# The first block of the second layer in a two-layer graph kernel: six columns by TensorE ahead of the loop, nineteen by gather, and another order of the vector engine's first steps

## The reference, cut to what matters

```python
# layer 0: an edge network
ew  = (efeat @ W_e + b_e).reshape(E, in_f, out_f)
msg = einsum('ei,eio->eo', feat[src], ew)
neigh = segment_sum(msg, dst) / maximum(cnt, 1) + bias
x = layernorm(x + neigh)
# layer 1: a typed message and a GRU
msg = einsum('emh,eh->em', edge_emb[edge_type].reshape(-1, 16, 16), x[src])
m = segment_sum(msg, dst)
x = layernorm(x + gru(m, x))
```

## Time and profile before

| | |
|---|---|
| median of 3 runs | 4953.85 us (4951.73 to 4953.85) |
| the profiled execution's own time | 4951.33 us |
| its span, first to last instruction | 4949.5 us |
| mean granted TensorE clock | 0.995 |
| busy: PE, VectorE, ScalarE, GpSimd | 4801.9, 4057.1, 4048.1, 3499.9 us |
| layer 0, then the change of layers, then layer 1 | to about 2466, to about 2516, to the end |

### The profile page before, as it was taken

How to read it: one execution, slowest core, us unless ns; L and a number is a source line. 1 busy time by engine, 2 the same in 40 slices (tenths; PEclk the granted TensorE clock), 3 DMA queues, 4 the chain that set the end, 5 groups by cost and what they waited for, 6 DMA issues and landing times.

```text
span 4949.5 us, 133716 instructions
## 1 busy us (share of the span) xinstructions
PE 4801.9 (97%) x40480; PEld 4330.9 (88%) x40481; DVE 4057.1 (82%) x5504; ACT 4048.1 (82%) x5764; POOL 3499.9 (71%) x3682
## 2 busy tenths in 40 slices
PE   6999999999999999999979999999999999999997
PEld 5888888888888888888869999999999999999997
DVE  8888888888888888888867777777777777777776
ACT  7888888888888888888658888888888888888885
POOL 7777777777777777777666767676767676767674
PEclk9999999999999999999989999999999999999999
DMA  3221221221111211112221111111111111111111
GB/s 75 35 37 34 37 35 35 37 34 35 37 34 35 37 34 35 37 34 35 33 34 28 27 28 27 28 27 28 27 28 27 28 27 28 27 28 27 28 27 16
DMA packets 371461, 159.41 MB, mean 32 GB/s; under 512 B 232707, under 2 KB 370531, under 8 KB 371291
## 3 DMA queue, kind: packets, MB, share of 16 engines
q1 hardware_dynamic: 254584, 127.93, 11.4%
q0 software_dynamic: 116672, 30.10, 7.8%
q10 hardware_dynamic: 160, 0.80, 0.1%
HBM read 155.84 MB, written 2.66 MB: 32 GB/s over the span
## 4 chain that ended last, share of the span: by engine, by line
PE 84%; DVE 10%; issue 4%; DVEq 1%; POOL 1%; DMA 0%; ACT 0%; SPq 0%; POOLq 0%; ACTq 0%
PE psN L703 66%; PE psM L733 13%; DVE z L900 4%; DVE cand L871 4%; PE psTR L724 1%; PE psTR L728 1%; PE psTR L725 1%; DVE z L875 1%; PE psTR L713 1%; POOL z L461 1%; DVE grp_hot L862 0%; PE psTR L717 0%; PE psTR L714 0%; DVEq L874 0%; PE psN L816 0%
## 5 line engine op out<-in xcount | busy, mean ns | idle before, releaser
L703 PE MATMUL psN<-table_hi,pick 128*128 128x320 f32 (+1 forms) x13020 | 3879.7, 315 | 45.9 <-DVEq L843 31.2
L703 PE MATMUL psN<-table_lo,pick 128*128 128x320 f32 (+1 forms) x13020 | 3769.9, 305 | 0.0
L703 PEld LDWEIGHTS psN<-table_hi,pick 128*128 128x128 f32 x13020 | 2447.5, 188 | 224.4 <-issue 171.9
L703 PEld LDWEIGHTS psN<-table_lo,pick 128*128 128x128 f32 x13020 | 2450.2, 188 | 0.0
L461 POOL DMA_INDIRECT z<-in_x,idx x1885 | 1798.6, 954 | 658.2 <-issue 471.4
L461 POOL DMA_INDIRECT z<-h_rows,idx x1761 | 1682.9, 956 | 708.5 <-issue 475.9
L520 ACT ACTIVATE dist<-src_mod,neg_node 128x640 bf16<-128x640 uint16 (+1 forms) x2480 | 2000.0, 844 | 64.8 <-ACT pick L528 54.8
L528 ACT ACTIVATE pick<-dist,one 128x640 fp32r<-128x640 bf16 (+1 forms) x2480 | 2003.9, 846 | 23.0 <-PE psN L703 6.8
L900 DVE TENSOR_TENSOR z<-psD,z 128x2048 f32<-128x2048 f32 (+1 forms) x750 | 1367.4, 1823 | 102.2 <-issue 57.9
L871 DVE TENSOR_TENSOR cand<-psN,grp_hot 128x640 f32<-128x640 f32 x1364 | 1075.8, 789 | 434.4 <-PE psN L703 364.8
L875 DVE TENSOR_REDUCE z<-cand 128x32 f32<-128x640 f32 x1364 | 1077.6, 790 | 132.0
(11 more groups left out here) (107 smaller groups left out, 681.4 us busy)
## 6 DMA issues: line engine op xcount, KB each, us to landing
src_mod<-src_mod_rows SPq DMA_DIRECT2D x372, 160.0 KB
z<-in_x,idx POOLq DMA_INDIRECT x1885, 2.3
z<-h_rows,idx POOLq DMA_INDIRECT x1761, 2.3
eab<-in_edge_attr SPq DMA_DIRECT2D x125, 200.0 KB
src_mod<-src_mod_rows SPq DMA_DIRECT2D x124, 192.0 KB
idx<-in_src SPq DMA_DIRECT2D x250, 12.5 KB
dstb<-in_dst SPq DMA_DIRECT2D x250, 14.0 KB
grp<-src_grp SPq DMA_DIRECT2D x248, 5.5 KB, 1.6
```

What stands on the lines that cost most here:

```text
L703: mm = pe.matmul(rows[:, :, 0:cells.shape[2]], pick[j][:, c, at:at + P], cells, start=(i == 0 and part == 0), stop=(i == TC - 1 and part = ...
```

## The change

Layer 1's block 0 no longer gathers all of its columns. The picks of turns 5 to 10 (`PICKED[5:11]`: columns 14, 21, 22, 23, 24 and 20, six of them) are made by TensorE; turns 0 to 4 are still passed over, and their five columns are gathered with the other fourteen: nineteen gathers in place of 25. The diff's `MADE_0` is the number of turns passed over. SyncE loads the source numbers for it (`load_first`) after the last block of layer 0 is picked. ScalarE's `begin()` makes `pick1` of block 0 in place of `pick0` of block 1, which moves to the head of layer 1's `first_body`. TensorE does the six turns of block 0, then eight turns of block 1 (`FIRST_S` goes from 11 to 8), `sum_block(0)`, and three more turns. VectorE does `group_hot` of block 0 and `split_table` ahead of `match_block`, then four selects of block 0, `group_hot` of block 1, and fewer selects of block 1 between the `outer` parts. `H`, `HCUT`, `PAIRS`, `GATHERED` and the `AFTER` tables are now given by buffer as well as by layer, with equal values for both; the counts that the loops wait for are worked out by `ahead`, `picked_of` and `cand_of`. Layer 0 keeps its schedule.

```diff
-H = (10, 11)
+H = ((10, 10), (11, 11))
-FIRST_S = (8, 11)
+FIRST_S = (8, 8)
+HALF_1 = 5
+MADE_0 = (H[0][0], HALF_1)
+FIRST_GATHERED = [[[g for g in range(START[j], START[j + 1]) if g not in PICKED[m:h[0]]] for j in range(NS)] for m, h in zip(MADE_0, H)]
+FIRST_PAIRS = [(5, 6), (6, 8), (8, 10)] + ([(10, 11)] if H[1][0] == 11 else [])
...
+        def ahead(k, buf, r):
+            return sum(H[k]) * r + buf * H[k][0]
+        def picked_of(k, buf, r, n):
+            return ahead(k, buf, r) + H[k][1] + n
+        def cand_of(k, buf, r, n):
+            return ahead(k, buf, r) + RING + n
...
+            def load_first():
+                at = slice(HALF_1 * P, H[1][0] * P)
+                sp.dma_start(src_mod[0][:, at], mod_dram[0:1, at].rearrange("a n -> (a n)").partition_broadcast(P)).then_inc(s_first, 16)
+                sp.dma_start(grp[0][:], grp_dram[0:1, :].rearrange("a (p t) -> (a p) t", p=P)).then_inc(s_first, 16)
...
             load_src(1, 1, 1)
+            sp.wait_ge(L[0]["pick_act"], TC * NH * NB + 1)
+            sp.wait_ge(L[0]["hot_g"], NB)
+            load_first()
             sp.wait_ge(s_agg[0], 1)
...
-                        for g in range(START[j], START[j + 1]) if whole else GATHERED[k][j]:
+                        for g in (FIRST_GATHERED[k] if first else GATHERED[k][buf])[j]:
...
-                                    pool.wait_ge(l["picked"], H[k] * (b + 1) + AFTER_OWN[k][n] + 1)
+                                    pool.wait_ge(l["picked"], picked_of(k, buf, r, AFTER_OWN[k][buf][n] + 1))
...
                 def begin():
                     if k == 0:
                         copy_coef(0, 0, 0)
-                    whole_half(1, 1, 0, 0)
+                        whole_half(1, 1, 0, 0)
+                    else:
+                        whole_half(0, 0, 0, 1)
 
                 def first_body():
+                    if k == 1:
+                        whole_half(1, 1, 0, 0)
                     whole_half(1, 1, 0, 1)
...
                 def first_body():
                     pe.wait_ge(s_split, k + 1)
+                    for t in range(MADE_0[k], H[k][0]):
+                        pick_rows(0, 0, 0, t)
                     for t in range(FIRST_S[k]):
-                        pick_rows(1, 1, t)
+                        pick_rows(1, 1, 0, t)
...
-                    dve.wait_ge(l["picked"], H[k] * (b + 1) + t1)
+                    dve.wait_ge(l["picked"], picked_of(k, buf, r, t1))
...
-                    dve.wait_ge(l["cand"], H[k] * b + t1 + RING)
+                    dve.wait_ge(l["cand"], cand_of(k, buf, r, t1))
...
                     else:
+                        group_hot(0, 0, 0)
+                        split_table(1)
                         match_block(0, 0, 0)
+                        for t0, t1 in FIRST_PAIRS:
+                            select(0, 0, 0, t0, t1)
                         group_hot(1, 1, 0)
-                        split_table(1)
+                        outer(0, 0, 0, 0)
                         selects(0)
-                        outer(0, 0, 0, 0)
-                        selects(1, 2)
                         outer(0, 0, 0, 1)
-                        selects(3, 4)
+                        selects(1)
                     outer(0, 0, 0, 2)
                     dve.sem_inc(l["rel_x"], 1)
                     dve.sem_inc(l["match_x"], 1)
-                    selects(*(range(2, len(PAIRS[k])) if k == 0 else range(5, len(PAIRS[k]))))
+                    selects(*range(2, len(PAIRS[k][1])))
...
-                dve.sem_inc(l["picked"], 2 * H[k])
-                dve.sem_inc(l["pick_act"], TC * NH + 1)
+                halves = NH if k == 0 else 1
+                dve.sem_inc(l["picked"], picked_of(k, 0, 0, MADE_0[k]))
+                dve.sem_inc(l["pick_act"], TC * halves + 1)
```

More of the change, by code:

```diff
@@ L21 @@
 PICKED = [4, 5, 6, 7, 13, 14, 21, 22, 23, 24, 20]
-H = (10, 11)
-HM = max(H)
-SCUT = [[sum(p < START[j] for p in PICKED[:h]) for j in range(NS + 1)] for h in H]
-HCUT = ((0, 5, 10), (0, 5, 11))
+H = ((10, 10), (11, 11))
+HM = max(max(h) for h in H)
+SCUT = [[[sum(p < START[j] for p in PICKED[:h]) for j in range(NS + 1)] for h in hs] for hs in H]
+HCUT = [[(0, 5, h) for h in hs] for hs in H]
 NH = 2
@@ L29 @@
 FILL = 24
-FIRST_S = (8, 11)
+FIRST_S = (8, 8)
 S_AT, T_AT, R_AT = (4, 1), (5, 3), (6, 5)
[L32 to L36, removed]
+GATHERED = [[[[g for g in range(START[j], START[j + 1]) if g not in PICKED[:h]] for j in range(NS)] for h in hs] for hs in H]
+assert all(2 * n % RING == 0 and n >= max(hs) for n, hs in zip(TURN, H))
+HALF_1 = 5
+MADE_0 = (H[0][0], HALF_1)
+FIRST_GATHERED = [[[g for g in range(START[j], START[j + 1]) if g not in PICKED[m:h[0]]] for j in range(NS)] for m, h in zip(MADE_0, H)]
+FIRST_PAIRS = [(5, 6), (6, 8), (8, 10)] + ([(10, 11)] if H[1][0] == 11 else [])
+assert all(c[1] == HALF_1 for c in HCUT[1])
+PAIRS = [[[(t, min(t + 2, h)) for t in range(0, h, 2)] for h in hs] for hs in H]
+AFTER_OWN = ([{3: 0, 5: 1, 6: 2, 7: 3, 8: 4, 12: 5, 13: 6}] * 2, [{5: 0, 6: 1, 9: 2, 10: 3, 11: 4, 12: 5}] * 2)
+AFTER_LAST = ([{1: 8, 2: 9}] * 2, [{1: 7, 2: 8, 3: 9, 4: 10}] * 2)
 SUB = 4
@@ L444, in gathers, with body @@
                 l = L[k]
-                def body(b, buf, r, whole=False):
+                def body(b, buf, r, first=False):
                     pool.wait_ge(l["idx"][buf], 16 * (r + 1))
@@ L464, in body @@
                             ).then_inc(l["got"][buf][j], 16)
-                body(0, 0, 0, whole=True)
+                body(0, 0, 0, first=True)
                 with pool.Fori(0, (NB - 1) // 2) as i:
@@ L684, in bank, with pick_rows @@
                     return (TURN[k] * buf + t) % RING
[L686 removed]
+                def pick_rows(b, buf, r, t):
+                    j = max(j for j in range(NH) if HCUT[k][buf][j] <= t)
+                    at = (t - HCUT[k][buf][j]) * P
                     if t >= RING:
[L689 to L696 removed]
+                        pe.wait_ge(l["cand"], cand_of(k, buf, r, t - RING + 1))
+                    else:
+                        last = max(u for u in range(H[k][1 - buf]) if (u - t - TURN[k]) % RING == 0)
+                        pe.wait_ge(l["cand"], cand_of(k, 1 - buf, r - 1 + buf, last + 1))
                     for i, c in enumerate(CHUNKS):
@@ L760, in first_body @@
                     sum_block(0)
-                    for t in range(FIRST_S[k], H[k]):
-                        pick_rows(1, 1, t)
+                    for t in range(FIRST_S[k], H[k][1]):
+                        pick_rows(1, 1, 0, t)
                     flush_transposes(first)
@@ L987, in body @@
                         outer(*nxt, 1)
-                    selects(*range(3, len(PAIRS[k])))
+                    selects(*range(3, len(PAIRS[k][1 - buf])))
                     if more2:
```

62 lines of the change are left out of this document (31 added, 31 removed).

## The result

The changed kernel takes 4941.0 us (median of 12 runs, 4939.95 to 4942.86); the kernel before, on the same chips, 4953.98 us (median of 12, 4950.91 to 4957.92). The ratio is 0.9974, 95% interval 0.9966 to 0.9983: 13.0 us faster. The forecast was 4949.7 us, the range began at 4945.5, and a gain over 0.2% had 2%. So it was wrong, in size. The profiled executions are 4951.33 and 4942.38 us, spans 4949.5 and 4940.6: 8.95 us apart. The one of before lies 2.65 us under its median, the one of after 1.38 us over its own; together these make the missing 4.0 us. The experiments ran on other chips, in three groups; beside them the kernel before had medians of 4953.65, 4953.88 and 4953.92 us, so the groups can be compared within some 0.3 us.

What follows compares the result with a forecast made beforehand. Gathers bounded layer 1's start up to block 1's sum; afterwards VectorE's closing work would, bringing that sum from 2556.52 to 2552.4. Gain 4.1 us, 4.2 with rounding: 4953.85 - 4.2 gives 4949.7 us, range 4945.5 to 4954.5.

Steps and rivals of the forecast that it cites:

- The head of the stage: VectorE at layer 1's start: split begins 1.27 us earlier, ends at 2514.5; TensorE's first pick at 2514.7.
- The turns: TensorE's fourteen turns before block 0's sum: 4.4 us at half clock, ending 2537.3; register loads add 0.5 us.
- VectorE's tail: VectorE's work after turn 9 of block 1, the new bound: 9.9 us, block 1's sum at 2552.4, 4.1 us earlier.
- Rival (a): Layer 1's start: gathers stay the bound and all 7.5 us arrive, 4946.3 us; chance 14%.
- (b): Layer 1's start: six added turns and selects cost what the gathers gave, 4953.9 up to 4955 us; chance 18%.
- this case: The main forecast for layer 1's start: gain 4.1 to 4.2 us, 4949.7 us, alone 4947.5 to 4951; chance 61%.
- ScalarE: `begin` takes 8.8 us in place of 7.3, covered by 4 us; block 1's `pick1` close, costed at nothing, at most 1 us.
- GpSimd and the split: Gathers beside VectorE's table split: 2.1 us slowdown left in place; by the port rule, nothing to 4.7 us.
- The clock in the gaps: TensorE's wait before block 1's sum: about 3.5 us; if the clock doesn't fall, 1.4 us more saved.
- The step that failed: Layer 1's two-block loop: bounded by TensorE and VectorE, its period and register operations unchanged by the change.
- rival (c): Loop waits for `picked` and `cand` each need one more register operation: 15 us slower, 4964.7 us; chance 4%.
- Rival (d): Layer 1's loop, moved in memory by new code, is fetched again each pass: 30 us slower, 4980 us; chance 1%.

Runs made afterwards that it cites:

- dense table: Window counts copied once into a dense table of 16-bit words and read from there: 5016.57 us on the changed kernel, 5025.75 us on the kernel before.
- one and three signals ahead: Changed kernel with strided 16-bit reads, plus one or three unused VectorE signals before the first block: 5016.92 us and 5024.9 us.
- strided table: Here the kernel before, with strided 16-bit reads and block 0's five surplus part-2 gathers counted on their own semaphore: 5019.79 us.
- The pair with the surplus gathers apart: Kernel before with dense 16-bit table, without and with block 0's five surplus part-2 gathers on their own semaphore: 5025.75 and 5020.97 us.

## Why the prediction was wrong, point by point

**The head of the stage: the order right, the start 1 us late.** The split was to end at 2514.5 and the first pick to start at 2514.7; the pick started at 2515.77. The timeline of VectorE of after has the new order, but 1 us later than I had it:

```profile
2510.47 0.37 DVE L895 TENSOR_TENSOR grp_hot<-col_f,grp 128x220 f32<-128x220 f32 x1
2510.76 1.69 DVE L870 CAST table_hi<-table 128x1280 fp32r<-128x1280 f32 x2
2512.49 3.01 DVE L872 TENSOR_TENSOR table_lo<-table,table_hi 128x1280 fp32r<-128x1280 f32 x2
```

In before `group_hot` started at 2510.72 behind `match_block`; here the copies of the node table that precede it ended 1.0 us later (in this execution TensorE's granted clock was also at half from 2492.5 to 2495.9 us, where before had it full), which ate 1.0 of the 1.27. The profile of before was itself an early one for the gathers: its first gather of layer 1 starts 40.2 us behind the last part-2 multiplication of layer 0, in the other three profiles with the old start 41.2 to 42.7 us. One reading of the earlier trace rows was also too short. The chain of before isn't gathers alone up to the sum of block 1; between the two sums it holds TensorE's work, among it turns of block 2:

```profile
2544.36 3.12 PE psN L703 x20
```

The gathers run beside this 1.26 us apart without a wait, so the sums made from them stand.

**The turns: right, and partly by luck.** Fourteen turns were to take 22.6 us and took 22.21. One window of after (us, busy of PE, PEld, DVE, ACT, POOL, PEclk, DMA, GB/s):

```profile
2519.00:2520.00 1.00, 1.00 (x6) 1.00 (x6) 0.82 (x2) 0.44 (x1) 0.69 (x2) 0.61 0.58 117
```

The clock came back 4.0 us after the first turn began, where I had taken 4.4 and bounds of 3.3 and 5.8. The sum of block 0 starts at 2537.98, forecast 2537.8, but two misses cancel in that: the start was 1.1 us later, the turns 0.4 us cheaper, and the 0.5 us for TensorE's register loads were nothing. The load ran beside the turns:

```profile
L312 PEldq TENSOR_LOAD <-span_row x1: 538/538/538, 2535.3 to 2535.3; - x1
```


**VectorE's tail: right.** 9.9 us were to lie between turn 9 of block 1 and its sum; from 2542.72, where the chain leaves TensorE's turns for VectorE, to 2552.82 there are 10.1. Forecast for that sum 2552.4, measured 2552.82, against 2556.52: 3.7 us gained, 4.1 forecast. Rival (a) is out: the tail, not a gather, stands ahead of that sum. So is (b): block 2's part-2 multiplication is 3.67 us earlier. VectorE's own register load of 0.81 us, in the chain at 2546.44, had no term in this tail; it runs beside part 0's multiplication (2547.09 to 2548.31) and so adds nothing here. Its place in the loop is another matter. (The bounds that I gave for this case, 4947.5 to 4951, come out of their own terms as 4947.3 to 4950.3.)

**ScalarE: right.** Its `begin` ended ahead of the normalisation, and the picks of block 1's second half came about 1 us later than worked out, as the first turn did, without a wait on TensorE. In its timeline of after:

```profile
2478.05 0.93 ACT L554 ACTIVATE pick<-dist,one 128x768 fp32r<-128x768 bf16 x1
2483.43 0.47 ACT L676 ACTIVATE z<-z 128x320 f32<-128x320 f32 x1 [4.44 <-POOL z L504]
...
2532.43 0.94 ACT L554 ACTIVATE pick<-dist,one 128x768 fp32r<-128x768 bf16 x1
```

4.44 us of cover are left (forecast 4), and TensorE has no wait for a pick up to 2537.98.

**GpSimd and the split: the traces decide for a cost that stays.** The first two slowed gathers lie over the cast and the subtraction, the third, at 2515.91, just behind them. They cost 1.0, 1.5 and 0.1 us above an ordinary one of 0.95, 2.6 us in all, against 2.1 in before; in the fourteen profiles it is 1.9 to 2.6 us. That is within the 0 to 4.7 us that I had worked out from the port rule of the Trainium skill ("SBUF — State Buffer", on the shared port pair) and the length of the split. They don't lie on the path now.

**The clock in the gaps: mis-sized, known as a bound.** The sum of block 0 took 1.65 us against 3.18, that of block 1 2.13 against 3.08. I had given up to 1.4 us for it and left it out of the sum. A window of before, in its second stretch at half clock, with TensorE idle:

```profile
2555.00:2556.00 1.00, 0.00 (x0) 0.00 (x0) 1.00 (x1) 0.00 (x0) 0.82 (x1) 0.50 0.12 10
```

And one of after, behind the sum of block 1:

```profile
2554.00:2555.00 1.00, 1.00 (x18) 0.57 (x7) 1.00 (x4) 0.00 (x1) 0.73 (x1) 0.50 0.57 112
```

In before TensorE stood still for 4.3 us up to 2539.05 and from 2547.5 to 2556.5, and the clock was at half from 2538.9 to 2542.3 and from 2552.6 to 2559.4. In after it works on to 2548.8 with two gaps of 0.4 and 0.6 us and stands still from there to 2552.8, 4.1 us (forecast 3.5); the clock holds at full from 2519.8 to 2553.9, and then falls all the same, for 3.4 us. In this profile it is neither of my two cases for this gap, then, but one between them. In three others with the new start and an unchanged loop (dense table, one and three signals ahead) the clock doesn't fall here at all, and the sum of block 1 takes 1.69 us: there the whole 1.4 us arrived. Of the three other profiles with the start of before, one (strided table) has stretches at half as long as before's, 3.4 and 6.8 us; the two with the dense table have longer ones, 10.2 or 13.7 us and then 10.2 us. In the kernel before with the dense table they run from 2540.6 to 2550.9 and from 2554.3 to 2564.5. One window of these:

```profile
2542.00:2543.00 1.00, 1.00 (x25) 1.00 (x21) 0.99 (x4) 0.00 (x0) 0.69 (x2) 0.50 0.81 90
```

From layer 0's last part-2 multiplication to that of block 2, the four profiles with the old start show 112.6, 114.1, 116.9 and 117.3 us; five with the new start and no other edit inside layer 1's loop (but the reads) 108.9, 110.0, 108.0, 108.2 and 107.5. So the start is worth 3.8 us in the pair of before and after and 6.7 on the mean of these nine. Two things go with the dearer profiles of the old start: its gathers begin later, which the new start, with the gathers off its path, doesn't feel, and its stretches at half clock are longer. With 6.3 us from the loop that makes the 13 us of the medians. What the runs without a profile did in this stage wasn't seen, so this split of the remaining 4 us is an estimate from nine profiles.

**The step that failed** is the sentence "the two-block pattern behind it is bounded by TensorE and VectorE and has no clock of its own", together with "the same two-block period from then on, with as many register operations at each wait", and rival (c)'s reason "the values are the same as before". I priced layer 1's loop at nothing because the change adds no work to it; it gave 6.3 us. Without that the forecast of a gain of 4.2 us would have met one of about 6.7, and 4947.3 us lies in the range. But the values weren't the same: one wait's value lost its 80. I had looked at register operations at the waits that the diff rewrites (`picked`, `cand`), and only for a loss; the line that waits for gathers is untouched, but its value comes from `got_of`, which the change rewrites (in a part of the diff that isn't shown above) and feeds with block 0's shorter list of gathers, and the sign was a gain. In the whole pass VectorE's register operations even rose, from 61 to 62, the additional ones at places where its sequencer is ahead of its arithmetic. Rival (c) had the right mechanism with the wrong sign, and half the price: it took an operation at the 40 ns of its row, and in the pass it is 0.08 us. Over 60 passes the operation makes 4.9 of the 6.3 us, the pauses among the additions the other 1.3. What was missing was a row: one of VectorE's sequencer between the freeing of the buffer and the next multiplication, which would have told that this list has no slack.

**Rival (d)**, the loop's place in the code, was looked for in the wrong unit. The loop isn't fetched again through a queue: 27 and 19 packets for 60 passes. But a shift by one instruction moved the pass by 0.09 us, three by 0.20, without anything in those queues. In the changed kernel's own trace, and in that of before, the head of the pass has no such pause (0.05 us between the last register operation and the multiplication in both), so the change didn't pay or gain there. The 0.02 us of its 0.105 that came among the additions are of this kind, pauses between the same instructions, but no run shifted the code of either kernel with its 32-bit loads, so that they come from the place of the code is an inference.

## What to carry to other kernels

When a pass is repeated sixty times, look at the sequencer's rows of the engine that comes last before the bound, and count what stands there one instruction at a time: here a register operation or a signal was 0.08 to 0.10 us of path, a register load 0.8 us and more. A constant that changes in a wait's value can add or remove such an operation with no line of the loop touched, so compare the values, not the lines. And move register loads to where the engine waits anyway: here that was worth another 9.8 us, three quarters of what the change gave, and 82 us between two kernels with the slow loads.

## What the runs showed of the hardware that I had not expected

- A load of six registers from SBUF on VectorE's sequencer takes 0.81 us from 32-bit words and 1.39 us from 16-bit halves, dense or strided. Where the sequencer is late it lies on the path one for one (0.579 us a load more, 0.58 us a block more). A load of two registers on TensorE or ScalarE got no longer by 16-bit reads (537 to 521 ns, 492 to 474 ns).
- A bare signal on VectorE takes 21 ns by its row and 0.09 to 0.10 us of the path; a register operation takes 40 to 45 ns and 0.08 us.
- The place of a loop in the code matters by pauses of 0.09 to 0.11 us at fixed instructions, the same in all 55 passes measured: 39.127, 39.217 and 39.331 us for zero, one and three instructions ahead. Their position moves with the code, and they cost only where the sequencer is late. What makes them stays open; the instruction queues have 27 and 19 packets in all three kernels. Two variants that differ in their instructions can't be compared below 0.1 to 0.2 us a pass without a look at where these pauses fall. The pair with the surplus gathers apart was compared instruction by instruction for that reason.
